# A Flamingo block's feed-forward on one core: the second pass multiplies h by w2 as seven turned Strassen products

## What is computed

```python
h = gelu(einsum('nd,edh->neh', xf, w1) + b1)        # xf: layernorm(x), 1792 x 512; w1: 8 x 512 x 1024
y = einsum('neh,ehd->ned', h, w2) + b2              # w2: 8 x 1024 x 512
out = (y * norm_g[:, None, None]).sum(axis=1)       # norm_g: one number per token, from the gate
x = x + tanh(g_ffn[0]) * out
```

## Time and profile before

| what | value |
|---|---|
| median of 3 runs | 1821.08 us (1820.44 to 1821.96) |
| the profiled execution's own time | 1821.18 us |
| its span, first to last instruction | 1819.4 us |
| granted TensorE clock, mean | 1.000 |
| busy: TensorE | 1796.5 us, 99% |
| busy: VectorE | 1234.7 us, 68% |
| busy: ScalarE | 869.9 us |
| busy: GpSimd | 1164.1 us, 64% |

### The profile page before, as it was taken

How to read it: one execution, slowest core, us unless ns; L and a number is a source line. 1 busy time by engine, 2 the same in 40 slices (tenths; PEclk the granted TensorE clock), 3 DMA queues, 4 the chain that set the end, 5 groups by cost and what they waited for, 6 DMA issues and landing times.

```text
span 1819.4 us, 31887 instructions
## 1 busy us (share of the span) xinstructions
PE 1796.5 (99%) x9720; PEld 1617.9 (89%) x9720; DVE 1234.7 (68%) x2056; ACT 869.9 (48%) x1700; POOL 1164.1 (64%) x900
## 2 busy tenths in 40 slices
PE   8999999999999999999999999999999999999999
PEld 7999999999999878888888888888888888888887
DVE  6888888888888866565655555577665656565647
ACT  6767677677766843333333424344333333333333
POOL 5525445263544679676767676699877676777743
PEclk9999999999999999999999999999999999999999
DMA  5111102021120222212121111122311111212111
GB/s 171 44 37 40 57 20 63 20 63 40 34 69 16 92 97 70 70 46 69 47 68 51 64 57 59 47 72 97 128 59 59 57 63 52 68 47 69 46 47 52
DMA packets 52057, 110.35 MB, mean 61 GB/s; under 512 B 13208, under 2 KB 25496, under 8 KB 52000
## 3 DMA queue, kind: packets, MB, share of 16 engines
q1 hardware_dynamic: 52000, 109.64, 18.6%
HBM read 98.61 MB, written 11.01 MB: 60 GB/s over the span
## 4 chain that ended last, share of the span: by engine, by line
PE 96%; DVE 2%; ACT 1%; issue 1%; DMA 0%; SPq 0%; ACTq 0%; DVEq 0%
PE bank L800 33%; PE scores L772 29%; PE bank L634 20%; PE scores L705 5%; PE bank L715 4%; PE bank L727 4%; PE bank L641 1%; DVE xs L921 0%; PE scores L858 0%; DMA ctx_raw<-in_ctx 0%; ACT hs L1387 0%; DVE acc L1094 0%; ACT probs L1280 0%; DVE hs L921 0%; DVE h_sum L1067 0%
## 5 line engine op out<-in xcount | busy, mean ns | idle before, releaser
L800 PE MATMUL bank<-w2s,hs 128*128 128x512 f32 x2688 | 630.9, 390 | 2.3 <-DVE acc L1094 1.2
L800 PEld LDWEIGHTS bank<-w2s,hs 128*128 128x128 f32 x2688 | 504.3, 188 | 102.9 <-DVE acc L1094 1.6
L772 PE MATMUL scores<-xs,w1s 128*128 128x448 f32 x2646 | 558.5, 366 | 3.7 <-ACT h_sum L1236 1.6
L772 PEld LDWEIGHTS scores<-xs,w1s 128*128 128x128 f32 x2646 | 496.3, 188 | 51.3 <-issue 3.2
L921 DVE TENSOR_TENSOR hs<-h_full,hs 128x448 fp32r<-128x448 f32 x256 | 272.3, 1064 | 196.6 <-ACT hs L1387 195.5
L1236 ACT ACTIVATE h_sum<-scores 128x448 f32<-128x448 f32 x189 | 103.1, 545 | 607.6 <-PE scores L772 607.6
L1094 DVE TENSOR_TENSOR acc<-bank,acc 128x512 f32<-128x512 f32 x337 | 225.0, 686 | 48.2 <-PE bank L800 46.1
L1079 DVE TENSOR_TENSOR h_sum<-scores,h_sum 128x448 f32<-128x448 f32 x189 | 117.9, 624 | 169.1 <-PE scores L772 121.0
L1476 POOL TENSOR_SCALAR probs<-probs,row_inv 112x750 f32<-112x750 f32 x60 | 130.7, 2179 | 99.2 <-DVE row_inv L1010 99.2
L1386 ACT ACTIVATE h_full<-h_sum,b1T 128x448 f32<-128x448 f32 x193 | 128.8, 668 | 120.1 <-DVE h_sum L1079 81.1
L1578 POOL CAST w1s<-w_stage 128x768 fp32r<-128x768 f32 x64 | 53.7, 839 | 202.1 <-PE scores L772 202.1
(11 more groups left out here) (130 smaller groups left out, 2302.3 us busy)
## 6 DMA issues: line engine op xcount, KB each, us to landing
w_stage<-in_L_ffn_w SPq DMA_DIRECT2D x128, 512.0 KB, 3.5
ctx_raw<-in_ctx SPq DMA_DIRECT2D x16, 376.0 KB, 3.1
ctx_raw<-in_ctx SPq DMA_DIRECT2D x14, 374.0 KB, 3.0
xa<-in_x SPq DMA_DIRECT2D x16, 224.0 KB, 2.7
xres<-in_x SPq DMA_DIRECT2D x16, 224.0 KB, 2.7
x_scratch<-xres SPq DMA_DIRECT2D x16, 224.0 KB, 2.3
xt_scratch<-yT SPq DMA_DIRECT2D x16, 224.0 KB, 2.8
x_raw<-xt_scratch SPq DMA_DIRECT2D x4, 896.0 KB, 8.1
```

The lines of the kernel that those rows point to most:

```text
L772: mm = pe.matmul(product_bank(g, name)[:, 0:TH], w1s[j % 2][:, s, W_OF[name], kc, :], xs[:, i, m, kc, :], start=opens and n == 0, stop=n == 5,
L800: mm = pe.matmul(bank[:, :], hs[j % 2][:, s, ht, t * P:(t + 1) * P], w2s[j % 2][:, m, ht, :], start=n == 0, stop=n == 5)
```

## The change

Pass 1 computes what it did. Pass 2 is changed in its second half and in its weights.

- **Turned Strassen.** The product is y transposed = w2 transposed x h. w2's slice (256 hidden x 512) is a 2 x 2 block matrix, h too (two hidden blocks x two token halves). Seven products (`SECOND`) replace eight. Each has two output halves of 128 rows, so there are 14 groups (NZ) of three matmuls with 448 columns (`second_t`), w2 as the stationary operand. Four groups of products are added onto a bank that already holds another product (`SECOND_ONTO`). A bank can therefore be continued only when VectorE has added what it held before; the adds (`add_t`, 14 a step) go to `acc_t`, which holds y transposed. Two groups stand after the fifth product of the next step, twelve after the seventh.
- **Sums of h.** T1 to T4 are differences of the blocks of h, made by VectorE (`h_difference`), rounded by ScalarE (`h_sum_high`) and given low parts by VectorE (`h_sum_low`). The low parts of the three blocks used directly (B21, B11, B22) move to GpSimd (`h_direct_low`). B12 is only used in sums and loses its second Gelu.
- **Sums of w2.** GpSimd makes four sums of 256 columns (`add_w2`), splits three direct blocks (`split_w2_direct`) and the four sums (`split_w2_sums`).
- **w1.** In pass 1 SyncE stores each split w1 (128 x 3584 float32, 1.8 MB) to memory, and rereads it in pass 2. GpSimd no longer splits w1 there.
- **The end.** After the last add, TensorE turns y tile by tile (`turn_y`, four transposes each), and VectorE forms gate x y + x2 from the bank (`result_t`). b2 is turned once at the start of the pass (`turn_b2`) and added with the first add. x2 is loaded over a w1 buffer. Several SBUF tiles now share addresses with tiles that pass 1 alone needs.

The diff's core:

```diff
+SECOND = {"P1": ("A11", "B11"), "P2": ("A12", "B21"), "P3": ("S4", "B22"), "P4": ("A22", "T4"), "P5": ("S1", "T1"),
+          "P6": ("S2", "T2"), "P7": ("S3", "T3")}
+SECOND_ORDER = ["P1", "P2", "P6", "P5", "P7", "P3", "P4"]
+SECOND_LAST = ["P2", "P1", "P5", "P6", "P7", "P4", "P3"]
+SECOND_BANK = {"P1": 0, "P6": 0, "P7": 0, "P4": 0, "P2": 2, "P5": 2, "P3": 2}
+NZ = 2 * len(SECOND)
+Z_AMONG = 2
...
+            def store_w1(g):
+                p, e, j = g
+                sp.wait_ge(w1_split, upto(2, g, 2))
+                sp.dma_start(w1_scratch[e, j], w1s[j % 2][:, :, :, :, :].rearrange("p s m c n -> p (s m c n)").bitcast(F32)
+                             ).then_inc(w1_stored[j % 2], 16)
...
+            def second_t(g, order, k):
+                name, m = order[k // 2], k % 2
+                w, h = SECOND[name]
...
+                if m == 0:
+                    if h in POOL_H_LOWS:
+                        pe.wait_ge(h_pool_lo, since_turn(3, g, POOL_H_LOWS.index(h) + 1))
+                    else:
+                        pe.wait_ge(h_sum_lo, since_turn(4, g, H_LOWS.index(h) + 1))
+                same = [i for i, of in enumerate(order) if SECOND_BANK[of] == SECOND_BANK[name]]
+                at_ = same.index(k // 2)
+                if at_:
+                    pe.wait_ge(z_added, since_turn(NZ, g, 2 * same[at_ - 1] + m + 1))
+                elif not at(g, (1, 0, 0)):
+                    pe.wait_ge(z_added, since_turn(NZ, g, 0))
...
+            def sums_t(g, before, i):
+                if i == 0 and before:
+                    h_sum_low(before, "T1")
+                    h_difference(before, "T4")
+                elif i == 1:
+                    block_sum(g, "C11")
+                elif i == 2 and before:
+                    for name in ("T3", "T2", "T4"):
+                        h_sum_low(before, name)
+                elif i == 4:
+                    block_sum(g, "C22")
+                    if before:
+                        for k in range(Z_AMONG):
+                            add_t(before, SECOND_ORDER, k)
+                elif i == 6:
+                    block_sum(g, "C12")
+            def tiles_t(g, before):
+                for k in range(Z_AMONG, NZ):
+                    if before:
+                        add_t(before, SECOND_ORDER, k)
+                    if k in (3, 6, 9):
+                        h_difference(g, {3: "T1", 6: "T3", 9: "T2"}[k])
...
                 for i in range(NM):
                     hidden(g, i)
+                    if p and i == 0 and not at(g, (1, 0, 0)):
+                        h_sum_high(previous(g), "T4")
...
-                if not at(g, (0, 0, 0)):
+                if p:
+                    add_w2(g)
+                    split_w2_direct(g)
+                    h_direct_low(g, "B21")
+                    split_w2_sums(g)
+                    h_direct_low(g, "B11")
+                    h_direct_low(g, "B22")
+                elif not at(g, (0, 0, 0)):
                     split_w2(g)
```

330 lines of the change are left out of this document (280 added, 50 removed).

## The result

The changed kernel takes 1841.35 us, median of 4 runs (1837.42 to 1843.95), against 1821.52 us (4 runs) for the kernel before on the same chip: a ratio of 1.0109, 95% interval 1.0093 to 1.0126. It is slower by 20 us; the forecast was 1845.9 us, 24.7 more. The profiled execution took 1843.95 us with a span of 1842.1, which is 22.7 more than the span before; it is the slowest of its four.

A forecast was written before the change was run, and what follows sets the result against it. TensorE was taken to set the pace, 18.05 us a step. Steps +10.9, results +3, gate +3.5, end +8.3 and turn -1 gave +24.7, a span of 1844 and 1845.9 us with 1.8 around it; range 1806 to 1876.

The forecast's parts named there:

- The sum: Whole kernel: steady steps +10.9, results +3, gate +3.5, end +8.3, turn -1, together +24.7 us.
- What TensorE gains: Second half of pass 2 steps: matmuls of 448 columns for 512, 17.01 us a step, 1.04 less, 32 us at most.
- The steady step: Full steps of pass 2: 18.4 us each for 18.05, +10.9 us over 31 steps.
- The walk: One pass 2 step followed through the engines' queues: 0.5 us lost at P7, 0.8 in the tail.
- (a): First steps of pass 2: seven result operations of pass 1, hidden before, now stand before adds and C22; +3 us.
- (b): The gate's 16 small operations come ahead of C22 on VectorE and stall P3; +3.5 us.
- (c): End of the kernel: last 14 adds, transposes and seven results follow the last products; +8.3 us.
- (d): Turn between the passes: GpSimd no longer splits w1 there, the bias must be turned; -1 us.
- (e): Stores and rereads of w1, 1.8 MB, one each a step: hidden, so nothing; +9 if each were late by 0.3 us.
- Rival 4: Pass 1: w2 queues behind the stores on SP's queue, GpSimd's split is late; 1855 us, chance 0.06.
- Rival 1: Pass 2: TensorE stays the bound, 17.1 us a step, 1802 us; needs under about 0.8 us waited; chance 0.16.

The follow-up runs named there:

- e3: Changed kernel with GpSimd's pass 2 operations cut to 8 columns after the first two steps, y not computed in full; 1804.25 us, 0.9916 of before.
- e10: Changed kernel with ScalarE keeping P1 ahead of the roundings T1, T3 and T2 in step (1,0,1); 1840.73 us, 1.0115 of before.
- e7: Changed kernel with the first two products of a second half waiting only for the add that last used their own bank; 1840.75 us, 1.0102 of before.
- e4: Kernel before with split w1 stored in pass 1 and reread in pass 2, without GpSimd's split there; 1819.10 us, 0.9995 of before.
- e6: Changed kernel with the edits of e1, e2 and e5 together; 1812.36 us, 0.9954 of before.
- e2: Changed kernel with VectorE's differences T3 and T2 moved behind adds 9 and 11, from 6 and 9; 1821.43 us, 1.0006 of before.
- e5: Changed kernel with all seven result operations of pass 1 placed in step (1,0,0); 1841.75 us, 1.0101 of before.
- e1: Changed kernel with ScalarE's rounding of T4 moved behind its keeping of U2; 1830.93 us, 1.0053 of before.
- e9: Changed kernel with the edits of e1, e2 and e7, pass 1's results spread over four steps, and P1 kept ahead of three roundings; 1812.61 us, 0.9946 of before.

## Why the prediction was right, and where it was not

The side and the mechanism came out: VectorE, sharing SBUF with GpSimd, gives back what TensorE gains, and the end costs some 8 us. The sum was +24.7, the medians differ by 19.8 and the spans of the profiled executions by 22.7. But the two largest misses were in opposite directions, and the clock, which the sum leaves out, cost the profiled execution some 3 us in F and T. So the closeness of the total is partly luck.

- **What TensorE gains.** Right. The pitch of the second half is 0.2025 us, and a step without contention 17.10 (e3) for 17.01 forecast.
- **The steady step, 18.4 against 18.08.** Mis-sized: +10.9 forecast for 31 steps, about +1 measured (S, +0.7 in 24). The walk gave VectorE 2.3 us behind at the start of a step (measured 2.2), T4 ready at 4.1 us (4.4), U2 kept at 5.3 (5.5) and P7 0.5 us late (0.7). That half was right and a little too small. The tail was forecast to lose 0.8 and lost 0.25. What was wrong was to give T1 and T3 a wait of 0.6 and 0.4 us in the tail as if GpSimd were always in the way. T1 takes 0.64 us, undisturbed, and T3 0.89. The mean of the eight operations is 0.82 us, below the 0.9 to 1.1 that I named, and the 3.5 us waited in a step are 1.6. VectorE is busy for 84% between 1300 and 1700 us, not over 90.
- **(a) The results, +3.** Mis-sized, the largest miss: the three steps that hold them and (1,1,0) cost 9.1 us more than before, some 1.5 of it by the clock (1302.49, six matmuls in 2.58 us for 1.47). In the changed kernel TensorE waits 1.74 us at 1261.61 for an add, behind T1 at 1258.03, which took 2.84 us beside GpSimd's 2.39. I had priced the seven operations and not that, each late, they push the two-SBUF operations behind them into GpSimd's long ones. And TensorE waits 2.46 us for P1 of (1,0,1), a place that I had not walked: I took the steady step's queue for the first one's. e10 shows that this wait moves with ScalarE's order and does not go; it comes from VectorE's differences, which stand in a row there with no adds between them.
- **(b) The gate, +3.5.** Right within 1: G is 1.7 longer, and (1,7,3) 1.0, 2.7 in sum. P3 does wait for C22 behind the gate (1.34 us at 1791.04); a wait of 1.53 us for an add behind T3, which took 2.44 us, I did not forecast.
- **(c) The end, +8.3.** Right: 21.4 us for 13.0, +8.4. Within it two misses cancel: the results are over 18.1 us in, not 19.0, and 3.3 us follow them, not 2.5. e3 and e7 show that it is VectorE's own queue: with GpSimd's operations on 8 columns, or without TensorE's first wait, it is 21.4 us too.
- **(d) The turn, -1.** The turn itself, (0,7,3) to (1,0,0), is 28.9 us for 30.3: -1.5 (28.2 to 28.9 in the other changed kernels). e4 has -2.2 without the bias to be turned.
- **(e) Stores, 0.** Right: P is the same to 0.25 us (e4: 0.1). Rival 4 is out. F's +2.9, which the sum does not have, is not theirs: e4 and six others with the stores have 28.4.
- **Rivals.** Rival 1 (TensorE stays the bound, 17.1 a step) is what e6 shows when three orders are changed; it gives 1812, not 1802, since ends and gate stay. Its condition, less than about 0.8 us waited in a step, was too strict: e6 waits 1.2 us at 17.17, and e2 0.9 us at 17.37. Where the waits stand decides.

**What stays open.** F differs between kernels whose pass 1 is the same (28.4 in seven, 28.8 before, 29.5 to 31.7 in four). In the changed kernel the first low part of h on VectorE met GpSimd's 2.37 us operation from its start; in the kernel before GpSimd was 1 us ahead:

```profile
667.82 2.37 POOL L1860 TENSOR_TENSOR w2s<-w_stage,w2s 128x1024 fp32r<-128x1024 f32 x1 [0.18 <-POOL w2s L1857]
667.93 2.74 DVE L1070 TENSOR_TENSOR hs<-h_full,hs 128x448 fp32r<-128x448 f32 x1 [2.39 <-ACT hs L1626]
```

Before, that operation took 1.84 us. All twelve traces divide by which of the two starts first. In the seven with F at 28.4 VectorE starts 0.10 to 0.48 us ahead and its operation takes 0.62 to 0.78 us; in the other five GpSimd is first, and it takes 1.84 to 2.80. What sets who is first is not shown by a run; an edit of pass 2 alone does not lengthen F, since e2 and e5 have one too. The other 1.6 us of F in the changed kernel are the clock's (below).

## What to carry to other kernels

Price a swap of TensorE time for VectorE time by contention and by where the operations stand, not by their sum: the same eight operations cost 5.0 us a step with GpSimd's cut to 8 columns, and 5.9 to 7.0 beside the full ones, and moving two of them by two or three places was worth 20 us in 1841. Walk the first and the last steps of a loop on their own, each engine's queue in turn; here they held nearly all of the loss. And after one order is mended look at who is late next before calling it small: e1 and e2 apart reached 1831 and 1821, together (with e5's edit, which gained nothing alone) 1812. Before a difference of 1 or 2 us between two traces is put down to an edit, compare their granted clocks: e9's gain in T and a third of e10's were the clock's.
